# A transformer layer in split float16: probabilities and attention result turned by DMA instead of on TensorE, and normalised after attention

## The reference

```
x = x + layernorm(attention(layernorm(x)))     # 32 heads of 128, 8 key/value heads, causal, rotary
x = x + layernorm(ffn(layernorm(x)))           # down(silu(gate(x)) * up(x)), 1376 hidden columns
attn = softmax(q k^T / sqrt(128) + causal mask);  out = attn v;  result = out @ dequant(o_codes)
dequant(codes, scales) = (codes - 8) * scales, one scale for each 128 input rows and output column
```

## Time and profile before

| | |
|---|---|
| runs | 1669.48, 1672.84, 1672.77 us; median 1672.77 |
| profiled execution | 1673.2 us; span from first to last instruction 1671.4 us |
| PE busy over the span | 1590.2 us (95%), 10080 matmuls |
| DVE, ACT, POOL busy | 1343.2 (80%), 978.0 (59%), 826.4 us (49%) |
| mean granted clock of TensorE | 0.988 |
| DMA | 57.55 MB, mean 34 GB/s |
| attention loop, feed-forward part | until about 1424 us; the rest |

### The profile page before, as it was taken

The page is one execution under the profiler, slowest core; times in us unless marked ns, Lnnn a source line. Parts: engine busy times, 40 slices in busy tenths (PEclk is TensorE's granted clock), DMA queues, the critical chain, the costliest instruction groups (busy, mean ns, idle before and its releaser), DMA issues.

```text
span 1671.4 us, 36140 instructions
## 1 busy us (share of the span) xinstructions
PE 1590.2 (95%) x10080; PEld 896.7 (54%) x10080; DVE 1343.2 (80%) x3108; ACT 978.0 (59%) x2390; POOL 826.4 (49%) x962
## 2 busy tenths in 40 slices
PE   5799999999999999999999999999999996999998
PEld 3455555555555555555555555555555553444543
DVE  7788888788878887888788878887888889667744
ACT  3566666566666666666666666666666673322311
POOL 4466555555555555555555555555555552101100
PEclk9899999999999999999999999999999998899999
DMA  7105100000000000000000000000000001010100
GB/s 244 51 27 110 43 27 26 27 26 27 26 27 26 26 26 27 26 26 26 27 26 26 27 27 26 26 27 27 26 26 27 1 10 30 13 45 20 38 26 26
DMA packets 25965, 57.55 MB, mean 34 GB/s; under 512 B 2784, under 2 KB 4544, under 8 KB 25792
## 3 DMA queue, kind: packets, MB, share of 16 engines
q1 hardware_dynamic: 23328, 51.07, 9.4%
q0 software_dynamic: 2464, 4.23, 1.4%
HBM read 55.32 MB, written 4.19 MB: 36 GB/s over the span
## 4 chain that ended last, share of the span: by engine, by line
PE 90%; DVE 4%; issue 3%; DMA 1%; ACT 1%; POOL 1%; SPq 0%; DVEq 0%; POOLq 0%; ACTq 0%
PE ps_p L683 9%; PE ps_p L684 8%; PE ps_p L685 8%; PE ps_t L735 8%; PE ps_p L707 7%; PE ps_p L708 6%; PE ps_o L748 4%; PE ps_o L750 4%; PE ps_o L749 4%; PE ps_s L720 4%; PE ps_s L722 4%; PE ps_s L721 4%; PE ps_s L909 3%; PE ps_s L910 3%; PE ps_p L923 2%
## 5 line engine op out<-in xcount | busy, mean ns | idle before, releaser
L409 POOL TENSOR_SCALAR prob<-prob,inv_sum 128x512 f32<-128x512 f32 (+3 forms) x512 | 295.7, 578 | 543.4 <-DVE inv_sum L1016 508.9
L1000 DVE SCALAR_TENSOR_TENSOR y<-ps_p,wo_scale,y 128x512 f32<-128x512 f32 x512 | 371.3, 745 | 83.2 <-PE ps_p L708 79.2
L536 ACT ACTIVATE pt_hi<-ps_t 128x512 f16<-128x512 f32 (+3 forms) x512 | 198.9, 434 | 236.1 <-PE ps_t L735 236.1
L527 ACT ACTIVATE prob<-prob,exp_bias 128x512 f32<-128x512 f32 (+3 forms) x512 | 280.7, 550 | 34.0 <-DVE exp_bias L1010 33.8
L683 PE MATMUL ps_p<-x_hi,w_hi 128*128 128x512 f16 x640 | 247.7, 387 | 15.0 <-issue 6.3
L684 PE MATMUL ps_p<-x_lo,w_hi 128*128 128x512 f16 x640 | 247.1, 386 | 0.0
L685 PE MATMUL ps_p<-x_hi,w_lo 128*128 128x512 f16 x640 | 246.7, 385 | 0.0
L1010 DVE CUSTOM_DVE_ANT_0 prob<-ps_s,mask 128x512 f32<-128x512 f32 (+3 forms) x512 | 228.5, 485 | 16.3 <-PE ps_s L722 13.7
L1022 DVE TENSOR_TENSOR pt_lo<-ps_t,pt_hi 128x512 f16<-128x512 f32 (+3 forms) x512 | 225.7, 483 | 0.0
L399 POOL TENSOR_TENSOR rot<-rot,swap 128x512 f32<-128x512 f32 x160 | 203.7, 1273 | 15.2 <-DVE rot L978 1.4
L396 POOL TENSOR_TENSOR swap<-swap,sin 128x512 f32<-128x512 f32 x160 | 203.5, 1272 | 10.9 <-DMA wo_scale<-o_scales 3.1
(11 more groups left out here) (111 smaller groups left out, 2934.0 us busy)
## 6 DMA issues: line engine op xcount, KB each, us to landing
w_code<-w_codes SPq DMA_DIRECT2D x36, 384.0 KB, 3.0
w_scale<-w_scales SPq DMA_DIRECT2D x36, 384.0 KB, 3.9
o_code<-o_codes SPq DMA_DIRECT2D x35, 256.0 KB, 2.7
swap<-x SPq DMA_DIRECT2D x16, 256.0 KB, 2.6
out<-z SPq DMA_DIRECT2D x16, 256.0 KB, 2.0
ffn_w<-x SPq DMA_DIRECT2D x3, 1024.0 KB, 9.4
ffn_w<-gate_t POOLq DMA_DIRECT2D x1, 1376.0 KB, 10.2
ffn_w<-up_t POOLq DMA_DIRECT2D x1, 1376.0 KB, 15.8
```

The lines of the kernel that those rows point to most:

```text
L409: pool.tensor_scalar(t, t, inv_sum[:, hp, i:i + 1], P_UP, ALU.mult, ALU.mult).then_inc(norm_done, 1)
L527: act.activation(prob[:, hp, P_AT[i]:P_AT[i] + w], prob[:, hp, P_AT[i]:P_AT[i] + w], ACT.Exp, bias=exp_bias[:, hp, i:i + 1], scale=-1.0, a ...
L1000: dve.scalar_tensor_tensor(tile, ps_p[:, bank, :], scale, tile, ALU.mult, ALU.add).then_inc(o_add, 1)
```

## The change

The transposes of the probabilities leave TensorE. Softmax is left unnormalised: `bias` adds ln(4096) to the row minimum, so that the exponentials come out scaled, ScalarE rounds all 1,280 columns of a head to float16 (`p_high`), GpSimd takes the rest (`p_low`), and SP starts a DMA transpose for each (`turn_p_hi`, `turn_p_lo`) into `pt_hi` and `pt_lo`, which are double-buffered in the space of the down weights. `attend` now has the turned probabilities as its stationary operand, in 30 matmuls of 128 columns, so that its result has the queries on partitions; VectorE multiplies it by the inverted sums, broadcast over 128 columns (`o_norm`), ScalarE and GpSimd split it (`o_high`, `o_low`), and two more DMA transposes (`turn_o`) turn it for `output`. `attend` moves to the start of the next iteration, and the output tiles are those of head n - 2. The four banks of `ps_t` and `ps_p` become one ring of four.

The rotary step changes too: VectorE multiplies by sin out of PSUM into `other`, SP swaps the halves by two DMA copies (`swap_halves`), GpSimd adds, and GpSimd takes the low part in VectorE's place. The dequantisation moves from GpSimd to VectorE, in one instruction. `o_code` has one buffer. The pieces are spread otherwise (`FULL`), and the down weights and `down_f` are loaded after the last attend.

```diff
-FULL = (("K",), ("V", "Q0"), ("Q1",), ("Q2", "Q3"))
+BLOCKS = PW // P
+RING = 4
+FULL = (("K", "V"), ("Q0", "Q1"), ("Q2",), ("Q3",))
 LAST = (("Y0",), ("Y1",), ("Y2", "X0"), ("Y3", "X1"))
...
+        ps_p = psum("ps_p", [P, RING, 512])
...
+        pts = ffn_w[:, 2 * KT * DFF:2 * KT * DFF + 4 * PW].rearrange("p (b k q) -> p b k q", k=BLOCKS, q=P)
+        pt_hi, pt_lo = pts[:, 0:2, :, :], pts[:, 2:4, :, :]
...
+            def swap_halves(V, vpar, piece):
+                buf = rope_index(vpar, piece) % 2
+                after(sp, rot_sum, rope_index(V, piece) - 1)
+                sp.sem_inc(sp_passed)
+                sp.wait_ge(other_done, rope_index(V, piece) + 1)
+                sp.sem_inc(sp_passed)
+                sp.dma_start(swap[0:64, buf, :], other[64:128, buf, :]).then_inc(swap_in[buf], 16)
+                sp.dma_start(swap[64:128, buf, :], other[0:64, buf, :]).then_inc(swap_in[buf], 16)
+            def turn_p_hi(n, hp):
+                after(sp, oq_ps, n - 1)
+                sp.sem_inc(sp_passed)
+                sp.wait_ge(p_hid, n + 1)
+                sp.sem_inc(sp_passed)
+                sp.dma_start_transpose(pt_hi[:, hp, :, :], p_hi[:, :]).then_inc(pt_hi_in, 16)
+            def turn_p_lo(n, hp):
+                sp.wait_ge(p_lod, n + 1)
+                sp.sem_inc(sp_passed)
+                sp.dma_start_transpose(pt_lo[:, hp, :, :], p_lo[:, :]).then_inc(pt_lo_in, 16)
+            def turn_o(n, hp):
+                after(sp, o_ps, (n - 1) * KT)
+                sp.sem_inc(sp_passed)
+                sp.wait_ge(oq_hid, n + 1)
+                sp.sem_inc(sp_passed)
+                sp.dma_start_transpose(ot_hi[:, hp, :, :], o_hi[:, :]).then_inc(ot_hi_in, 16)
+                sp.wait_ge(oq_lod, n + 1)
+                sp.sem_inc(sp_passed)
+                sp.dma_start_transpose(ot_lo[:, hp, :, :], o_lo[:, :]).then_inc(ot_lo_in, 16)
...
+            def unit(U, r, slots=FULL, first=False, more=True, last=False):
+                for h in range(HG):
+                    n = U * HG + h
+                    turn_p_hi(n, h % 2)
+                    if first and h == 0:
+                        swap_halves(0, 0, "Q3")
+                    else:
+                        for V, vpar, piece, bank, taken in made_before(U, r, h, slots):
+                            if piece != "V":
+                                swap_halves(V, vpar, piece)
+                    turn_p_lo(n, h % 2)
+                    if not (first and h == 0):
+                        turn_o(n - 1, (h - 1) % 2)
+                    if first:
+                        load_o(h + 1)
+                    elif h == 1 and not last:
+                        load_o(U + HG)
+                    if h == 1 and more:
+                        load_w(U + 6, r)
+                    if last:
+                        if h == 0:
+                            sp.wait_ge(rot_sum, len(ROPED) * UNITS)
+                        load_res(h)
...
+            def rope_add(V, vpar, piece, taken):
+                buf = rope_index(vpar, piece) % 2
+                pool.wait_ge(piece_dve, taken)
                 pool.sem_inc(pool_passed)
...
+                pool.wait_ge(swap_in[buf], swaps_landed(V, vpar, piece))
+                pool.sem_inc(pool_passed)
+                pool.tensor_tensor(rot[:, buf, :], rot[:, buf, :], swap[:, buf, :], ALU.add).then_inc(rot_sum, 1)
+            def rope_low(V, vpar, piece):
                 buf = rope_index(vpar, piece) % 2
...
-            def normalise(n, hp):
...
+                hi, lo = (k_hi[:, vpar, :], k_lo[:, vpar, :]) if piece == "K" else \
+                    (q_hi[:, int(piece[1]), :], q_lo[:, int(piece[1]), :])
+                pool.wait_ge(rot_hi, rope_index(V, piece) + 1)
                 pool.sem_inc(pool_passed)
...
+                pool.tensor_tensor(lo, rot[:, buf, :], hi, ALU.subtract).then_inc(rot_lo, 1)
+            def p_low(n, hp):
+                after(pool, pt_lo_in, 16 * n)
+                pool.sem_inc(pool_passed)
+                pool.wait_ge(p_hid, n + 1)
+                pool.sem_inc(pool_passed)
+                pool.tensor_tensor(p_lo[:, :], prob[:, hp, :], p_hi[:, :], ALU.subtract).then_inc(p_lod, 1)
+            def o_low(n):
+                after(pool, ot_lo_in, 16 * n)
+                pool.sem_inc(pool_passed)
+                pool.wait_ge(oq_hid, n + 1)
+                pool.sem_inc(pool_passed)
+                pool.tensor_tensor(o_lo[:, :], o_f[:, :], o_hi[:, :], ALU.subtract).then_inc(oq_lod, 1)
...
+                    n = U * HG + h
+                    p_low(n, h % 2)
                     if not (first and h == 0):
...
+                        o_low(n - 1)
+                    if first and h == 0:
+                        start_rope("Q3")
+                        rope_low(0, 0, "Q3")
+                    else:
+                        roped = [x for x in made_before(U, r, h, slots) if x[2] != "V"]
+                        for V, vpar, piece, bank, taken in roped:
+                            rope_add(V, vpar, piece, taken)
+                        for V, vpar, piece, bank, taken in roped:
+                            rope_low(V, vpar, piece)
...
+            def v_high(V, vpar, bank, taken):
+                act.wait_ge(piece_ps, taken)
+                after(act, oq_ps, (V - 1) * HG)
+                act.activation(v_hi[:, vpar, :], ps_p[:, bank, :], ACT.Copy,
+                               scale=O_UP / (X_UP * W_UP)).then_inc(v_hid, 1)
             def exps(n, hp):
...
-            def pt_high(n, g):
...
-            def ot_high(n, hp):
...
+                for done, i in enumerate(ORDER):
+                    a, w = P_AT[i], (i + 1) * P
+                    act.wait_ge(bias_done, n * NG + min(done, NG - 1) + 1)
+                    act.activation(prob[:, hp, a:a + w], prob[:, hp, a:a + w], ACT.Exp,
+                                   bias=exp_bias[:, hp, i:i + 1], scale=-1.0,
+                                   accum_out=exp_sum[:, hp, i:i + 1]).then_inc(exp_done, 1)
+            def p_high(n, hp):
+                after(act, pt_hi_in, 16 * n)
+                after(act, p_lod, n)
+                act.wait_ge(exp_done, (n + 1) * TT)
+                act.activation(p_hi[:, :], prob[:, hp, :], ACT.Copy).then_inc(p_hid, 1)
+            def o_high(n):
+                after(act, ot_hi_in, 16 * n)
+                act.wait_ge(oq_norm, n + 1)
+                act.activation(o_hi[:, :], o_f[:, :], ACT.Copy).then_inc(oq_hid, 1)
...
+                    if first and h:
+                        o_centre(h)
+                    if not (first and h == 0):
+                        o_high(n - 1)
                     if h == 3 and not last:
                         after(act, o_ps, outs_before(U) + 4)
...
+                        o_centre(U + HG)
                     if h == 2 and not last:
                         act.wait_ge(piece_ps, pieces_before(U))
                         w_high(U + 5)
...
+                    if not (last and h == HG - 1):
+                        exps(n + 1, (h + 1) % 2)
+                    if first and h == 0:
+                        rope_high(0, 0, "Q3")
+                    else:
+                        for V, vpar, piece, bank, taken in made_before(U, r, h, slots):
                             if piece != "V":
                                 rope_high(V, vpar, piece)
...
                     if not (last and h == HG - 1):
...
+                        p_high(n + 1, (h + 1) % 2)
+                    for V, vpar, piece, bank, taken in made(U, r, h, slots):
+                        if piece == "V":
+                            v_high(V, vpar, bank, taken)
...
-            def transposes(n, hp, g):
...
+            def attend(n, upar, hp, v_taken):
+                after(pe, oq_norm, n)
+                pe.wait_ge(pt_hi_in, 16 * (n + 1))
+                pe.wait_ge(pt_lo_in, 16 * (n + 1))
+                pe.wait_ge(piece_dve, v_taken)
+                for i in ORDER:
+                    o = ps_o[:, i * P:(i + 1) * P]
                     for j in range(i + 1):
...
-            def attend(n, U, upar, h):
...
+                        vh, vl = v_hi[:, upar, j * HD:(j + 1) * HD], v_lo[:, upar, j * HD:(j + 1) * HD]
+                        ph, pl = (part[:, hp, P_AT[i] // P + j, :] for part in (pt_hi, pt_lo))
+                        pe.matmul(o, ph, vh, start=(i == ORDER[0] and j == 0), stop=False)
+                        pe.matmul(o, ph, vl, start=False, stop=False)
+                        mm = pe.matmul(o, pl, vh, start=False, stop=(i == ORDER[-1]))
+                mm.then_inc(oq_ps, 1)
...
+                    if h:
+                        attend(n - 1, r, (h - 1) % 2, pieces_before(U - 1) + START.index("V") + 1)
+                    elif not first:
+                        attend(n - 1, 1 - r, 1, pieces_before(U - 2) + START.index("V") + 1)
                     if more:
                         scores(*nxt, 0)
...
-                    transposes(n, h % 2, 0)
```

(87 more changed lines are left out.)

519 lines of the change are left out of this document (206 added, 313 removed).

## The result

The changed kernel takes 1653.63 us (median of 4 runs, 1651.66 to 1655.17) against 1672.57 before: ratio 0.989, 95% interval 0.9873 to 0.9908. It is faster by 19 us, 1.1%; the forecast was 93 us, 1580. The profiled execution took 1652.42 (span 1650.6).

The account below looks back on a forecast made before the run. TensorE (PE) was taken to bound the loop, busy 781.66 of 800 us. From the profiled 1673.2: minus 139.5 for transposes, plus 5 for attend, 38 for waits and 3 for ends gave 1580 us, range 1550 to 1610.

Parts of the forecast that it names:

- What leaves PE, what it gets: TensorE loses ten f32 transposes a head, 139.5 us less; attend's 30 matmuls of 128 columns add 5 us.
- the rival without waits: In the loop, no wait is left: 1539 us, or 1524 with half of PE's idle time gone too; chance 0.15.
- The other engines as sums: Per unit, VectorE 30.2 us, ScalarE about 20, GpSimd 29.3, all under PE's 37.9, so they cost nothing as sums.
- The transfers: Four turning transfers a head priced by bytes: 2.9 us a head, landing 3.0 us for a p half, 2.5 for o.
- the rival of small dear runs: A turned 256-byte run costs like a packet: 29 us a head, near 4000 us; decides at 39 ns a run; chance 0.15.
- Where the loop waits: Before attend, one wait of 1.2 us a unit for the p_lo made at h = 2: 38 us in all.
- a cover of 2.8 us: Slack before attend for p_lo made in the three iterations other than h = 2: 2.8 us or more, no wait.
- the landing of the o halves: Before the outputs, over a whole iteration of time, so no cost; a stall only with landings over 5 us.
- Ends: Behind the last unit, one more attend, four output tiles and a 5 us chain, partly covered: +3 us; down_w's later load free.
- the last paragraph of the prediction: Signs to check; wrong if landings exceed 8 us, queue shares near 100%, or PE's clock falls because it waits.
- A late landing: p_lo lands late in the loop, 1816 us at a 10 us delay; chance 0.20, of which 0.07 still faster, 0.11 slower.
- D: Time from p_lo's low part made to its landing; decides at 7.8 us, through 13.3 + D = 2 x 10.53.

Follow-up runs that it names:

- all_together: Changed kernel with halves copied by ScalarE, its high parts before the last exponential, dequantisation at h = 0, no bias additions; 1574.19 us (0.9406).
- best_copies: all_together with the four turning transfers as plain copies of the same bytes, values wrong; 1511.42 us (0.9026).
- plain_copies: Changed kernel with the four transfers a head as plain copies without turning, values wrong; 1632.75 us (0.9751).

## Why the prediction missed

**What leaves PE, what it gets:** right in what it names; attend's matmuls start 0.056 us apart, as forecast from project_v. That the sum agrees, 36.95 us busy a unit against 36.9, is in part luck. all_together, at a clock of 1.00, is busy 562.66 us in the 15.7 units from 500 to 1100 us: 35.9 a unit, which is what the prediction's own iterations give (2 x 7.6 + 2 x 10.2 = 35.6). The forecast's 37.9 carried over 2.3 us of gaps of the old unit, of which only 1.0 was idle time; in after 0.8 us of lower clock took the place of the rest. For the same reason best_copies, at 1511, lies under 1539 and 1524, the two floors of the rival without waits.

**The other engines as sums:** near. VectorE 639.40 / 19.5 = 32.8 us a unit (30.2 forecast), ScalarE 21.3 (20), GpSimd 27.4 (29.3). What VectorE has more, by form in 500 to 1300 us:

```profile
L1113 DVE TENSOR_SCALAR exp_bias<-low 128x2 f32<-128x2 f32 x78 | 28.0, 359 | 11.6
L1025 DVE SCALAR_TENSOR_TENSOR w_lo<-w_scale,w_hi 128x768 f32 x19 | 25.4, 1338 | 0.0
L1035 DVE SCALAR_TENSOR_TENSOR w_scale<-w_code,w_scale 128x768 f32<-128x768 int32 x20 | 24.7, 1233 | 0.0
L1113 DVE TENSOR_SCALAR exp_bias<-low 128x1 f32<-128x1 f32 x156 | 24.0, 154 | 23.3
```

The dequantisation, forecast at 0.96 from the earlier trace rows, took 1.23. That row is from the start of the kernel. w_lo took 0.96 in the loop of before and 1.34 here; whether what GpSimd does beside them is the cause was not tried.

**The transfers:** the mechanism right, the size short. A run cost about 13 ns above the 12.8 by bytes, 26 in all, 5.9 us a head for 2.9: twice the value taken, under the 39 at which it would decide. So the rival of small dear runs fell, and with it the Trainium skill's 1309 ns for a 128x128 block (VectorE: DVE Perf Modes, § The three transpose paths) as a price for each block in turn: a half of p, ten blocks, lands in 3.5 us. Landings came at 3.5 to 4.1 us for 3.0, and 5.1 behind swaps and beside the o transfers. A transpose held SP's queue 1.2 to 2.0 us, where a copy's 0.33 had been taken.

**Where the loop waits: the step that failed.** It had one wait of 1.2 us, for the p_lo made in iteration h = 2 (with its own figures, 2 x 7.63 = 15.3, it is 1.0). That one is there, at 2.02. "The swaps ... cost p_lo nothing, since GpSimd ends later" was wrong: the four swap issues of Q0 and Q1 come just in front of the p_lo that GpSimd had ready 3.4 us earlier, and a second wait, 2.03, stands where a cover of 2.8 us had been counted. That cover was eaten by the queue, 3.4 us, and a landing 0.9 us longer. The four issues took 2.92 us, where 4 x 0.33 had been named and put at nothing. The idle time that this adds, 4.1 - 2.2 = 1.9 us a unit, is 32 x 1.9 = 61 of the 72 us between 1580 and the profiled 1652.4.

The chain to p_lo was also late before any transfer. Counted from attend's start at h = 2 (795.60): o_norm ends at 3.8 us (2.4 forecast), since VectorE still has the last piece's rotary step, an output tile and the dequantisation ahead of it; the last bias at 8.7 (6.3), p_hi at 12.0 (9.7), p_lo at 15.3 (13.3), and the landing adds 5.2 for 3.0: 20.5 where 16.3 was forecast. VectorE's late start on the head, 1.4 us, and its last bias, 0.74 us for 0.15, are most of the 2.4 at that point.

The step also followed only one chain. Q0's, from VectorE's lows and biases over the exps to q_hi, q_lo and the scores at h = 3, was never laid beside it. It hardly shows in after (9.2 us of waits in the window), since p_lo's comes first; it showed when p_lo's was cut (54.9, 60.9 and 41.1 us of waits in three kernels). It explains why neither cheap transfers nor a free queue brought the forecast time; the four edits on both chains brought 79 us. A third term put at nothing, the landing of the o halves, had a small price: 7.8 us of waits in the window of after, 17.6 in all_together.

**Ends:** +3 forecast; some 11 us were lost outside the steady loop, and one stall of 13.6, where the loads of gate_w and up_w meet the turns, covers it. The feed-forward part did not lengthen.

**The clock** fell as the last paragraph of the prediction feared (0.98 in the window, 0.97 over the span; 1.00 in the window of all_together), nine times in the window, each behind a wait. At 0.8 us a unit this is some 25 us over the loop, hidden in the comparison above by the gaps that the forecast had carried over.

**The rivals.** A late landing is what came true, in its mild form: still faster, with a chance of 0.07. The prediction's D runs from the low part made to the transfer landed, and so holds the queue too: in the unit shown it is 7.3 us (797.99 to 805.3) behind 12.6 for the head made at h = 1, and 5.2 behind 15.3 for the next. That is 19.9 and 20.5 us for two heads, where 21.06 would have left no gain. The medians of issue to landing, under 4.2, hide this. Not separated is what share of best_copies' 63 us is landing, and what SP's shorter issues.

## What to carry over

When work moves off the bounding engine onto a queue, list every chain that returns to that engine, each with its slack, and not only the one that the moved work is on; of three edits that eased p_lo's chain alone the best brought 21 us here, and edits on both chains 79. Price the issue of a transfer from the queue that must make it, with everything in front of it, and put tiny instructions and their waits on the list if several chains pass through them. Move an instruction ahead of others in an in-order queue only with its inputs: the same reordering won 27 us with an early input and cost some 94 with a late one.

## What the runs showed of the hardware

Turning 16-bit data by DMA in 128x128 blocks cost about twice a copy by bytes (26 ns a 256-byte run, over 16 engines), and 1.2 to 2.0 us of the issuing queue for each transfer. While a large load from GpSimd's queue ran, one turning transfer landed in 17.5 us and the issue of the next took 11.73, and with the load in four pieces PE waited up to 5.2 us; with plain copies its longest wait there was 2.6 us (plain_copies) and 3.7 (best_copies). The 128x2 bias took 0.74 us (start 803.60) beside GpSimd's add of 803.05 and 359 ns in the mean, the 128x1 a steady 154; why the two differ was not tried.
